# Nine wide pieces instead of sixteen narrow ones in the early score triangle of a channel attention

## The reference

```python
Q = (x @ Wq + bq).reshape(b, s, H, C) * inv_sqrt_c      # H = 16, C = 64
K = (x @ Wk + bk).reshape(b, s, H, C)
V = (x @ Wv + bv).reshape(b, s, H, C)
scores = jnp.einsum('bshq,bshk->bshqk', Q, K)
mask = jnp.triu(jnp.ones((C, C), dtype=bool), 1)
w = jax.nn.softmax(jnp.where(mask, -jnp.inf, scores), axis=-1)
attn = jnp.einsum('bshqk,bshk->bshq', w, V)
```

## Time and profile before

| what | before |
|---|---|
| median of three runs | 3630.36 us (3629.26 to 3630.54) |
| the profiled execution's own time | 3630.34 us |
| its span, first to last instruction | 3628.7 us |
| busy: PE, DVE, ACT, POOL | 87%, 65%, 55%, 38% of the span |
| mean granted clock of PE | 0.964 of 2.4 GHz |
| line 1449 POOL, line 1495 and 1509 DVE | 480 instructions each, 1019.7, 493.4 and 494.3 us |
| line 1418 ACT exponentials | 288, 406.7 us |
| line 1408 ACT exponentials of `own` | 2048, 708.0 us |

### The profile page before, as it was taken

One profiled execution on the slowest core, in us unless ns is written; L12 is line 12 of the kernel. 1 busy time (PEld: TensorE's weight loads), 2 busy tenths in 40 slices (PEclk: granted clock), 3 DMA queues, 4 the chain that ended last, 5 costly groups with the idle time before them and its releaser, 6 DMA issues. The chain is left out here.

```text
span 3628.7 us, 52641 instructions
## 1 busy us (share of the span) xinstructions
PE 3153.1 (87%) x19700; PEld 2195.5 (61%) x19700; DVE 2350.2 (65%) x4197; ACT 1979.3 (55%) x4488; POOL 1393.9 (38%) x1294
## 2 busy tenths in 40 slices
PE   4998988888799898888979889888897989988887
PEld 2566467776365646777536564777744656577773
DVE  3366379994246638999415653999931574499983
ACT  1546277773254628777226452877732654277763
POOL 0223077670031307776003120876501312276740
PEclk9999989999899998999989999999998999999999
DMA  4000100000200020000110001000011000100002
GB/s 132 1 1 1 55 7 1 1 1 24 71 1 1 1 61 1 1 1 1 61 33 1 1 10 53 1 1 1 1 61 33 1 1 18 44 1 1 1 1 64
DMA packets 69372, 68.51 MB, mean 19 GB/s; under 512 B 6077, under 2 KB 49623, under 8 KB 68970
## 3 DMA queue, kind: packets, MB, share of 16 engines
q1 hardware_dynamic: 60288, 56.15, 5.1%
q10 hardware_dynamic: 8810, 8.79, 0.8%
HBM read 63.88 MB, written 1.05 MB: 18 GB/s over the span
## 5 line engine op out<-in xcount | busy, mean ns | idle before, releaser
L1449 POOL TENSOR_TENSOR arena<-arena 128x1536 f32<-128x1536 f32 (+9 forms) x480 | 1019.7, 2157 | 401.3 <-DVE arena L1509 303.7
L1317 PE MATMUL psum<-ident,arena 128*128 128x128 f32 (+7 forms) x7168 | 869.7, 280 | 204.5 <-ACT arena L1418 201.7
L1317 PEld LDWEIGHTS psum<-ident,arena 128*128 128x128 f32 (+7 forms) x7168 | 794.4, 138 | 309.5 <-ACT arena L1418 263.6
L1408 ACT ACTIVATE arena<-arena 128x64 f32<-128x64 f32 (+7 forms) x2048 | 708.0, 485 | 136.3 <-PE psum L1326 136.3
L1509 DVE TENSOR_TENSOR arena<-arena,psum 128x1536 f32<-128x1536 f32 (+9 forms) x480 | 494.3, 1062 | 82.5 <-ACT arena L1418 74.8
L1495 DVE TENSOR_TENSOR arena<-arena,psum 128x1536 f32<-128x1536 f32 (+9 forms) x480 | 493.4, 1061 | 8.4 <-POOL arena L1449 6.5
L455 POOL TENSOR_SCALAR veps<-mv 128x1 f32<-128x1 f32 x128 | 24.7, 193 | 1192.3 <-DVE mv L450 1185.5
L1418 ACT ACTIVATE arena<-arena 128x1536 f32<-128x1536 f32 (+2 forms) x288 | 406.7, 1417 | 120.4 <-DVE arena L1495 120.4
L843 POOL TENSOR_SCALAR arena<-arena 128x512 f32<-128x512 f32 (+3 forms) x512 | 265.2, 536 | 498.9 <-DVE arena L806 498.8
L764 ACT ACTIVATE arena<-arena 128x512 f32<-128x512 f32 (+3 forms) x512 | 281.7, 552 | 184.5 <-DVE arena L799 184.5
L1095 PE MATMUL psum<-arena,stream 128*128 128x512 f32 x512 | 265.6, 601 | 5.0 <-DVE arena L1216 5.0
(11 more groups left out here) (222 smaller groups left out, 4222.5 us busy)
## 6 DMA issues: line engine op xcount, KB each, us to landing
stream<-in_L_ffn_W SPq DMA_DIRECT2D x160, 256.0 KB, 3.1
arena<-in_L_ffn_h_w SPq DMA_DIRECT2D x8, 1024.0 KB, 8.3
arena<-in_L_ffn_w_w SPq DMA_DIRECT2D x12, 256.0 KB, 4.6
arena<-in_L_ffn_h_w ACTq DMA_DIRECT2D x2, 1024.0 KB
wa<-in_L_attn_W_attn ACTq DMA_DIRECT2D x1, 1536.0 KB
wq<-in_L_attn_Wq ACTq DMA_DIRECT2D x2, 512.0 KB
wo<-in_L_attn_Wo ACTq DMA_DIRECT2D x2, 512.0 KB
x<-in_L_attn_x SPq DMA_DIRECT2D x4, 256.0 KB, 3.7
```

What stands on the lines that cost most here:

```text
L1317: last = nc.tensor.matmul(ps[ch.half][0:rows, to:to + P], buf[:, c:c + rows], ident[:], start=first, stop=False, is_transpose=True, skip_g ...
L1408: nc.scalar.activation(by_key[:, 0:HD - r, j], keys[:, h, 0:HD - r], ACT.Exp, bias=NB[:, j:j + 1], scale=Q3[tt % 2][:, j:j + 1]).then_inc( ...
L1449: last = nc.gpsimd.tensor_tensor(of_piece(D3[n % 5], piece), q, keys_on(K3[tt % 2], k, nk, w), ALU.mult)
```

## The change

In `score_chunks` the six early chunks get other pieces, each with a key count of its own. `rect` and `late` are written in the new form and stay as they are.

```diff
-    def pack(half, first_query, ragged, keys, starts):
+    def pack(half, first_query, ragged, pieces):
         at, out = 0, []
-        for k in starts:
+        for k, keys in pieces:
             w = HD // 2 - first_query - (k % (HD // 2) if ragged else 0)
             out.append((k, keys, w, at))
             at += keys * NH * w
         assert at <= CHUNK
         return Chunk(half, first_query, ragged, out, at)
 
-    early = [pack(1, 0, True, 2, starts) for starts in ((0, 16), (2, 14), (4, 12), (6, 10), (8, 18, 22), (20, 24, 26, 28, 30))]
-    rect = [pack(0, OWN, False, KB, (k,)) for k in range(0, HD // 2, KB)]
-    late = [pack(0, OWN, True, KB, starts) for starts in ((32,), (36, 52), (40, 48), (44,))]
+    early = [pack(1, 0, True, pieces) for pieces in (((0, 3),), ((13, 5),), ((9, 4),), ((3, 3), (29, 3)), ((6, 3), (26, 3)), ((18, 4), (22, 4)))]
+    rect = [pack(0, OWN, False, ((k, KB),)) for k in range(0, HD // 2, KB)]
+    late = [pack(0, OWN, True, pieces) for pieces in (((32, KB),), ((36, KB), (52, KB)), ((40, KB), (48, KB)), ((44, KB),))]
```

## The result

| | before | after |
|---|---|---|
| median on the chip | 3630.20 us (7 runs, 3629.26 to 3632.34) | 3643.02 us (7 runs, 3638.90 to 3645.15) |
| ratio, 95% interval | 1 | 1.0032 (1.0020 to 1.0043) |
| profiled execution: span | 3628.7 us | 3637.3 us |

The kernel became 0.3% slower, 12.8 us in the medians. The runs of after lie further apart than those of before, 6.3 us against 3.1.

A forecast was written before the change was run, and what follows sets the result against it. The prediction took ACT's exponentials to bound the early chunks of each channel-stage tile: +5.5 us for columns and +0.8 for TensorE's clock, +6.3 on 3630.34, gave 3636.6 us. Range 3632.4 to 3642 us.

The forecast's parts named there:

- the leg: First part of a channel-stage tile's chain of waits: ACT's exponentials run without a gap; DVE, POOL and PE wait for ACT.
- the term: ACT's changed exponential columns in that first part of a tile: +0.41 us for chunk 5, -0.05 for chunk 2, together +0.36 a tile.
- a sum of 5.5: Channel stage, ACT's columns: +5.8 us over 16 tiles and -0.3 in the passes' first tiles make +5.5 us.
- slow chunk 11: Channel-stage tile whose 24 PE matmuls at chunk 11 run at about 1.2 GHz: 0.77 us more; before, one of 12 tiles.
- the clock's term: TensorE's clock at chunk 11 of the channel tiles: +0.8 us taken, bounds -0.8 and +8.5.
- within 0.2%: Whole launch: no change to be told, 0.2% being 7.3 us; chance 0.58 in all, the forecast's own case 0.42 of it.
- rival 2: Slow clock reaches chunk 11 in more channel tiles, 0.77 us each; over 0.2% slower from three more; chance 0.38.
- three more tiles: Channel tiles slowed at chunk 11 beyond those before: at this number 5.5 + 2.3 = 7.8 us, over 0.2%.
- Rival 1: Across passes: each pass's +1.4 us is halved by the next, +2.6 us in all, 3633 us; chance 0.12.
- rival 3: Early chunks: DVE sets the pace and 14 fewer instructions a tile pay, a gain over 0.2%; chance 0.04.
- rival 4: Channel tiles: ACT's added columns are hidden; at most POOL's 0.14 us a tile shows, -2.2 us, 3628 us; chance 0.04.

The follow-up runs named there:

- pad_before: The kernel before with the exponential of chunk 5 run over 1536 columns instead of 1024, pieces unchanged: 3643.42 us, ratio 1.0036.
- short_after: The kernel after with the exponential of chunk 5 run over only the first 1024 of its 1536 columns: 3631.05 us, ratio 0.9999.
- the two kernels with both guards: Kernels after and before, each with idle matmuls ahead of the fills behind chunks 9 and 10 and in the sixth part's pause: 3631.09 and 3625.32 us.
- after_again: The kernel after, unchanged, run again for a second profile and more runs: 3641.66 us, ratio 1.0032.
- late_after: The kernel after with three more small ACT exponentials ahead of chunk 1's own ones in each pass's first tile: 3643.72 us, ratio 1.0035.
- moe_guard_after: The kernel after with seven idle matmuls of 128 columns in PE's 0.87 us pause in the sixth part: 3631.14 us, ratio 0.9999.
- late_before: The kernel before with three more small ACT exponentials ahead of chunk 1's own ones in each pass's first tile: 3641.15 us, ratio 1.0024.
- split_after: The kernel after with each of its nine early pieces cut in two on POOL and DVE, same columns: 3641.08 us, ratio 1.0030.

## Why the prediction was right and where it was wrong

**Right: the leg and the term.** ACT without a gap from chunk 2 to chunk 5, +0.41 us for chunk 5, +0.36 a tile (measured 93.40 to 93.75 and 93.77), nothing from DVE, POOL and PE. pad_before gives the columns alone, short_after the pieces alone, and the two kernels with both guards 5.8 us against a sum of 5.5. A first tile of a pass without a slow chunk 11 went from 93.20 to 93.59.

**Wrong: the size of the clock's term, and with it the case.** The step is "I take +0.8 us, one slow chunk 11 more than before and nothing absorbed". The medians lie 12.8 us apart instead of 6.3, so with 5.5 for the columns the clock's term measured 7.3 us, not 0.8. The profiled execution, a quick one, had four more slow chunks 11, +3.2 us, and lost 1.2 us more between the passes, where the forecast had no term; how the rest of the 7.3 us is shared out in the longer executions no profile of after shows. The measured 3643.0 us lies 1 us beyond the top of the range, and "within 0.2%" at 0.58 was the wrong side: the case that came is rival 2, at 0.38, slower by more than 0.2%. Its sign, its place and its price (0.8 us a tile, ACT's line 1390 waiting 1.71 us) are in the trace of after as it describes them; the point of three more tiles was passed with four, and reached in after_again.

**What rival 2 did not have.** It priced only chunk 11. late_after has 897.7 us a pass with hardly a slow chunk 11, and moe_guard_after takes the loss away from a place one part earlier. The forecast worked out its bounds from rows of the channel stage alone, though its own reason (every later instant moves) holds for every pause of PE in the pass.

**Rival 1, absorbed, was half of the truth.** A later arrival is partly made up, as rows 8 suggested; but what recurs is not half of the delay, it is the pass time. Delays of 1.4 us a pass (after), 1.6 (pad_before), 1.0 (late_before) and 2.4 (late_after) all give 897.4 to 897.8 us once a run is in that state, and 0 to 1.4 us a pass with pauses filled give 892.4 to 895.9. Halving does not tell when a kernel goes from one value to the other.

**Rivals 3 and 4** fell. Against rival 3, short_after gains nothing from nine pieces and split_after loses nothing with eighteen. Against rival 4, ACT's added columns were not hidden: in pad_before they alone make a plain tile 0.4 us longer.

**Still open.** Why the two values are 894.3 and 897.7 us, which of the slow stretches of a pass holds it at the second, and why the runs of after differ by 6 us. Those of the fifth part (at 3019 us in after) and of line 1112 alone do not, since short_after has both at 894.3 us, nor is a slow chunk 11 needed (late_after). The two kernels with both guards, 5.8 us apart instead of 12.8, show that what the columns do not explain comes through the clock; which instant is decisive was not isolated.

## What to carry to other kernels

Before merging instructions that work on padded shapes, ask which engine ends last in that stage and what it pays for: here it paid by the column, and the engines that paid by the instruction had been waiting for it. In a kernel whose PE has short pauses, a small delay can cost several times itself or less than itself: here 4.0 us cost 10.6 in one kernel and 0.7 to 2.1 in its neighbour. So a result of a few tenths of a per cent is judged as well against a version in which pauses of PE are filled: the two guarded kernels differ by 5.8 us, not 12.8. And filling those pauses can be worth more than the change in question; here it made the kernel before 5.4 us faster.

## What the runs showed of the hardware

- Seven idle matmuls of 128 columns in a 0.87 us pause brought the first x8 of matmul records behind it from 5.10 to 3.60 us and the launch from 3641.7 to 3631.1 us. Of TensorE's clock the Trainium skill (TensorE: Matmul & The Clock Gate, Part 1) says that it is a gate which activity opens and inactivity closes, and which does not follow the kernel's own start. The trace agrees that the pause alone does not decide: the same 0.87 us was followed by a granted clock of 0.50 in after and of 1.00 in before.
- Passes of this kernel mostly took about 894 us or 897.7 us. Three kernels with different amounts of added work (pad_before, late_before, late_after) took the second value in all their profiled passes, 897.62 to 897.75 us.
- 4.0 us of added ACT work cost 10.6 us in one kernel and 0.7 to 2.1 us in its neighbour.
- A slow stretch can be made good later in the pass: after lost 1.5 us at line 1112 and was still 1.1 us quicker than before from there to the channel stage, since its fills took 1.12 us where before's took 2.08.
